# Attention and mixture-of-experts layer: value products by head parity, and the last group's values in three parts

## The reference, cut to what matters

```python
attn = jnp.einsum('bqhmd,bkhd->bhmqk', q, k) * sm_scale
attn = jnp.where(mask, -jnp.inf, attn)
w = jax.nn.softmax(jnp.concatenate([attn, sink], axis=-1), axis=-1)[..., :-1]
out = jnp.einsum('bhmqk,bkhd->bqhmd', w, v).reshape(B, L, NQ * HD)
x = x + out @ W_out
...
x = x + experts(layernorm(x))      # 8 experts, top 2, capacity 640
```

## Time and profile before

| | us |
|---|---|
| median of 3 runs | 1070.48 (1070.36 to 1070.66) |
| the profiled execution | 1065.58 |
| its span, first to last instruction | 1063.8 |
| PE busy | 1032.3 (97%) |
| DVE busy | 918.9 (86%) |
| value matmuls of all groups, PE busy | 247.9 |
| value matmuls of the last group | 793.16 to 800.32 |

### The profile page before, as it was taken

The page is one execution under the profiler, slowest core; times in us unless marked ns, Lnnn a source line. Parts: engine busy times, 40 slices in busy tenths (PEclk is TensorE's granted clock), DMA queues, the critical chain, the costliest instruction groups (busy, mean ns, idle before and its releaser), DMA issues.

```text
span 1063.8 us, 32339 instructions
## 1 busy us (share of the span) xinstructions
PE 1032.3 (97%) x13013; PEld 729.8 (69%) x13013; DVE 918.9 (86%) x1962; ACT 653.7 (61%) x1670; POOL 663.4 (62%) x607
## 2 busy tenths in 40 slices
PE   6899999999999999999999999999998999999996
PEld 4466666666666666666666666666566999999995
DVE  6999999999999999999999999999966777677773
ACT  4676667666667666667776656777654455544451
POOL 5657776767666888666777877667762422233332
PEclk8999999999999999999999999999999999999998
DMA  3544555544333344333343344333324344454421
GB/s 94 150 114 117 129 135 130 137 118 131 95 84 81 95 110 105 97 100 79 80 111 101 95 131 111 94 86 98 100 80 159 87 121 121 126 125 124 101 44 21
DMA packets 115574, 112.11 MB, mean 105 GB/s; under 512 B 35264, under 2 KB 103936, under 8 KB 115296
## 3 DMA queue, kind: packets, MB, share of 16 engines
q1 hardware_dynamic: 97648, 90.29, 31.3%
q0 software_dynamic: 7296, 8.55, 5.0%
q10 hardware_dynamic: 10480, 11.20, 3.8%
HBM read 74.84 MB, written 21.83 MB: 91 GB/s over the span
## 4 chain that ended last, share of the span: by engine, by line
PE 60%; DVE 35%; issue 2%; ACT 1%; DMA 0%; SPq 0%; POOLq 0%; DVEq 0%
PE bank L1536 21%; DVE probs_ring L1124 15%; DVE probs_t L1133 13%; PE bank L1701 11%; PE bank L1512 11%; PE bank L1712 7%; DVE heads_sb L1153 4%; PE bank L1715 4%; PE bank L1568 1%; PE bank L1441 1%; PE bank L1676 1%; PE bank L1458 1%; PE bank L1476 1%; PE bank L1596 1%; DVE neg_max L1124 0%
## 5 line engine op out<-in xcount | busy, mean ns | idle before, releaser
L841 ACT ACTIVATE probs_ring<-probs_ring,neg_max 128x512 f32<-128x512 f32 x512 | 365.9, 717 | 210.2 <-DVE neg_max L1124 209.4
L1124 DVE CUSTOM_DVE_ANT_0 probs_ring<-bank,mask,sink_neg 128x512 f32<-128x512 f32 x512 | 360.3, 738 | 24.9 <-PE bank L1512 23.8
L1133 DVE STREAM_TRANSPOSE probs_t<-probs_ring 128x1024 f32<-128x1024 f32 x256 | 317.8, 1241 | 0.2 <-ACT probs_ring L841 0.2
L1512 PE MATMUL bank<-qk_st 64*128 64x512 f32 x1024 | 280.6, 624 | 11.6 <-DVE neg_max L1124 7.4
L1536 PE MATMUL bank<-probs_t,v_quads 32*64 32x256 f32 x8192 | 247.9, 381 | 0.0
L1536 PEld LDWEIGHTS bank<-probs_t,v_quads 32*64 32x64 f32 x8192 | 179.3, 132 | 75.4 <-issue 48.1
L670 POOL TENSOR_TENSOR chunk_sb<-chunk_sb,rope_sb 128x512 f32<-128x512 f32 (+1 forms) x94 | 119.8, 1275 | 111.1 <-issue 80.6
L789 POOL DMA_INDIRECT out<-expert_sb,slots x40 | 77.8, 1945 | 150.6 <-DVE expert_sb L1385 143.3
L1512 PEld LDWEIGHTS bank<-qk_st 64*128 64x128 f32 x1024 | 85.3, 185 | 77.0 <-DVE neg_max L1124 41.5
L1043 ACT ACTIVATE hidden<-bank,b_sb 128x320 f32<-128x320 f32 x128 | 60.5, 524 | 107.1 <-PE bank L1701 107.1
L675 POOL TENSOR_TENSOR qk_st<-chunk_sb,swap_sb 128x512 f32<-128x512 f32 (+1 forms) x94 | 120.0, 1276 | 7.4
(11 more groups left out here) (189 smaller groups left out, 1352.5 us busy)
## 6 DMA issues: line engine op xcount, KB each, us to landing
v_quads<-v_rows SPq DMA_DIRECT2D x128, 128.0 KB
recip_wide<-recip_rows SPq DMA_DIRECT2D x64, 256.0 KB
w_raw<-in_L_ffn_w SPq DMA_DIRECT2D x14, 1024.0 KB, 8.2
swap_sb<-chunk_sb SPq DMA_DIRECT2D x314, 32.0 KB
w_raw<-in_L_attn_W_qkv SPq DMA_DIRECT2D x32, 256.0 KB, 2.9
slots<-slot_rows SPq DMA_DIRECT2D x9, 662.5 KB, 4.0
slot_rows<-x2T ACTq DMA_DIRECT2D x8, 662.5 KB, 6.2
w_raw<-in_L_attn_W_qkv SPq DMA_DIRECT2D x64, 64.0 KB, 2.7
```

Source lines behind the costliest of these rows:

```text
L841: nc.scalar.activation(probs[(g * UNITS + n) % RING][:, :], probs[(g * UNITS + n) % RING][:, :], ACT.Exp, bias=neg_max[j][:, n:n + 1], sca ...
L1124: nc.vector.tensor_tensor_reduce(probs[(g * UNITS + n) % RING][:, :], SCORE[SCORE_OF[n // 2][n % 2]][:, :], mask[:, L - P - t * P:2 * L - ...
L1133: nc.vector.transpose(probs_t[j][:, :, (h // 2) * (2 * P):(h // 2 + 1) * (2 * P)] .rearrange("p b (h q) -> p h b q", h=2)[:, :, :, t * BLK ...
L1512: nc.tensor.matmul(SCORE[SCORE_OF[n // 2][hh]][:, :], qk_st[j][half, h // 2, t * P:(t + 1) * P], qk_st[j][half, PAIRS, :], start=True, sto ...
```

## The change

Column halves are now the head within a pair (parity `h`), and the columns of a result are the pairs `c`. The moving operand of a matmul is therefore two pieces of 128 columns, 256 columns apart, where it was one piece of 256. The reciprocals, the view in which DVE makes the heads, and the load of `W_out` follow that layout.

In the last group the values are made in three parts, in columns 256 to 511 of the PV banks: pair 0 for queries 0 to 63 (the first quarter of the work) after the scores of step 10; in step 20, after the old rows of bank 2, pair 0 for queries 64 to 127, and pair 1 whole. The old rows of banks 1 and 0 follow. Queries 0 to 63 here are columns 0 to 63 of the 128 in a quarter, which are query tiles 0 and 1.

```diff
-                                 w_out.rearrange(...)[:, k, 2 * p:2 * p + 2, :]
+                                 w_out.rearrange(...)[:, k, p:p + 3:2, :]
...
-                    nc.vector.reciprocal(recip[:, 0:UNITS].rearrange("p (c h t) -> p c t h", c=PAIRS, h=2),
+                    nc.vector.reciprocal(recip[:, 0:UNITS].rearrange("p (h c t) -> p c t h", c=PAIRS, h=2),
...
+                    cols = slice(2 * P, 4 * P) if g == GROUPS - 1 else slice(0, 2 * P)
...
-                            PV[a][:, 0:2 * P].rearrange("p (h t i) -> p h t i", h=2, i=BLK),
+                            PV[a][:, cols].rearrange("p (c t i) -> p c t i", c=PAIRS, i=BLK),
...
             def pe_ahead(m):
+                if m == LAST + 10:
+                    pe.wait_ge(s_turned, LAST // 2 + 2)
+                    pe.wait_ge(s_v_in[1], (GROUPS // 2) * (16 * QUADS))
+                    pe.wait_ge(s_heads, 2 * (GROUPS - 1) + 1)
+                    last_values(0, slice(0, HD))
...
+            def values(g, j, blk, pairs, cols, q=slice(0, P)):
+                c, d = divmod(blk, TPB)
+                for a in range(QUADS):
+                    rows = slice(a * BLK, (a + 1) * BLK)
+                    probs_of = probs_t[j][rows, blk, :].rearrange("k (c h q) -> k c h q", c=PAIRS, h=2)
+                    for h in range(2):
+                        ins = nc.tensor.matmul(PV[a][h * HD:(h + 1) * HD, cols], v_quads[j][rows, d, c * HD:(c + 1) * HD],
+                                               probs_of[:, pairs, h, q], start=(blk == 0), stop=(blk == BLOCKS - 1))
+                return ins
+
+            def last_values(pair, q):
+                first = (2 + pair) * P
+                for blk in range(BLOCKS):
+                    ins = values(GROUPS - 1, 1, blk, pair, slice(first + q.start, first + q.stop), q)
+                return ins
...
                         pe.wait_ge(s_old_in, 16)
-                        for bank in (2, 1, 0):
+                        pe.wait_ge(s_neg_max, GROUPS * UNITS - 2)
+                        old_rows(2)
+                        pe.wait_ge(s_turned, GROUPS * (UNITS // 2))
+                        pe.wait_ge(s_y_out, 2 * g)
+                        last_values(0, slice(HD, P))
+                        last_values(1, slice(0, P)).then_inc(s_pv, 1)
+                        for bank in (1, 0):
                             pe.wait_ge(s_neg_max, GROUPS * UNITS - bank)
                             old_rows(bank)
...
-                    for blk in PV_AT[n]:
...
+                    if g < GROUPS - 1:
+                        for blk in PV_AT[n]:
+                            ins = values(g, j, blk, slice(0, PAIRS), slice(0, 2 * P))
+                        if blk == BLOCKS - 1:
+                            ins.then_inc(s_pv, 1)
```

More of the change, by code:

```diff
@@ L903, in load_wo @@
                     act.dma_start(wo_sb[p * HD:(p + 1) * HD, 2 * k:2 * k + 2, :],
-                                 w_out.rearrange("(k m d) n -> d k m n", m=QM, d=HD)[:, k, 2 * p:2 * p + 2, :]
+                                 w_out.rearrange("(k m d) n -> d k m n", m=QM, d=HD)[:, k, p:p + 3:2, :]
                                  ).then_inc(s_wo_in[k % 2], 16)
@@ L1151, in dve_step @@
                         dve.wait_ge(s_y, 2 * g + 1)
+                    cols = slice(2 * P, 4 * P) if g == GROUPS - 1 else slice(0, 2 * P)
                     for a in range(QUADS):
                         ins = nc.vector.tensor_tensor(
-                            heads_sb[:, a, :].rearrange("p (h t i) -> p h t i", h=2, i=BLK),
-                            PV[a][:, 0:2 * P].rearrange("p (h t i) -> p h t i", h=2, i=BLK),
-                            recip_wide[:, a, :].rearrange("p (h t i) -> p h t i", h=2, i=BLK), ALU.mult)
+                            heads_sb[:, a, :].rearrange("p (c t i) -> p c t i", c=PAIRS, i=BLK),
+                            PV[a][:, cols].rearrange("p (c t i) -> p c t i", c=PAIRS, i=BLK),
+                            recip_wide[:, a, :].rearrange("p (c t i) -> p c t i", c=PAIRS, i=BLK), ALU.mult)
                         if a % 2 == 1:
@@ L1520, in pe_step @@
                         pe.wait_ge(s_old_in, 16)
-                        for bank in (2, 1, 0):
+                        pe.wait_ge(s_neg_max, GROUPS * UNITS - 2)
[5 more added lines that the diff above has]
+                        for bank in (1, 0):
                             pe.wait_ge(s_neg_max, GROUPS * UNITS - bank)
                             old_rows(bank)
-                    if PV_AT[n][0] == 0:
+                    elif PV_AT[n][0] == 0:
                         pe.wait_ge(s_turned, g * (UNITS // 2) + UNITS // 2)
```

## The result

The changed kernel takes 1083.77 us (median of 4 runs, 1079.9 to 1086.01), the kernel before 1070.42 in the same session: ratio 1.0129, 95% interval 1.0093 to 1.0165. It is slower by 13.4 us. The forecast was no change, and the result lies above its range. The profiled execution took 1079.90 us; its span is 14.3 above that of before.

A forecast was written before the change was run, and what follows sets the result against it. PE, busy 97% of the span, was taken as the bound. Groups nothing, quarter 0.85 us late, values ending 1.4 us earlier, old rows moved behind them: -0.1 us, 1070.48 to 1070.4, no change; range 1069.4 to 1076.5.

The forecast's parts named there:

- the pace of the short matmuls: Last group's values: 7.0 ns a record of 64 columns, 13.8 ns a record of 128, against 27.5 for 256.
- q: Time of 256 records of 64 columns, in the mid-group quarter and again in step 20: 1.8 us each.
- r: Time of the 128-column records, pair 1 whole, in step 20: 3.5 us.
- a sign of being wrong: Profile after: short records' starts over 11 ns apart on average would show the forecast wrong.
- the prediction's own formula: Total difference for other paces: -0.1 + 2 (q - 1.8) + (r - 3.5) us.
- The reason for 7.0: In the last values' first 60 ns 8 matmuls and 8 loads started, under 8 ns a pair; lower pace chosen.
- Groups 0 to 30: Moving operand read in two pieces of 128 columns: costs nothing, 1 us kept to either side.
- The quarter's price in DVE's time: Quarter ahead of step 12's scores: scores +1.24 us, unit 14's mask, last transposes and reciprocals 0.85 us late.
- The end: After last transposes: values end 798.8 instead of 800.2, Y at 801.16 instead of 801.24; gain 0.5 us at most.
- The clock: Idle 1.5 us added before last values, one filled at 784: no loss taken; a fall would cost 1.7 us.
- Rival 1: Last group: PE's queue issues one matmul per 27.5 ns, q = r = 7.0, +13.8 us, 1084.3; chance 0.12.
- Rival 2: Last group: load not hidden under 64 columns, or middling instruction rate; q = r = 4.2, +5.4 us, 1075.9; chance 0.17.

The follow-up runs named there:

- All wide: Changed kernel with the last group's same 384 matmuls each streaming 256 columns instead of 64, 64 and 128; 1083.39 us, ratio 1.0114.
- two pairs: Changed kernel without the mid-group quarter: in step 20 pair 0 whole, then pair 1 whole, 256 matmuls of 128 columns; 1078.15 us, ratio 1.0067.
- values twice: Kernel with only the layout by parity, the last group's undivided values done twice in a row; 1080.05 us, ratio 1.0075.
- layout only: Changed kernel keeping only the layout by parity; last group's values undivided, 256 columns wide, behind all old rows as before; 1070.05 us, ratio 0.9972.
- Quarter, then whole: Changed kernel's mid-group quarter with its result thrown away, then all old rows and undivided values at step 20; 1074.27 us, ratio 1.0039.
- old rows behind Y: Layout by parity, undivided values, no quarter; old rows of banks 1 and 0 behind Y replace three unused matmuls; 1069.61 us, ratio 0.9994.
- the old rows between: Changed kernel with the old rows of banks 1 and 0 between step 20's 64-column and 128-column parts; 1081.22 us, ratio 1.0081.
- half a quarter: Changed kernel whose mid-group quarter takes only the first 8 of 16 key blocks, 128 matmuls of 64 columns; 1079.79 us, ratio 1.0086.

## Why the prediction was wrong

**What failed is the step "the pace of the short matmuls"**, q = 1.8 us and r = 3.5 us, worked out from what a tile needs and carried over to streams of 256 records. Two things were wrong in it, and the larger was a wait that it had put at nothing without a reason.

- *The supply.* The step took for granted that PE always has its next instruction. The cut takes the last group's value records from 256 to 768, 512 of them in step 20, and halves or better the time of each, so a block that lasted 3.5 us is used in 1.4 to 1.8. The pauses from start to start are 1.92, 2.10 and 3.53, 7.6 us together. "All wide" shows that the columns don't decide, "two pairs" that the same columns in twice the instructions take twice the time, with pauses 128 records apart, and "values twice" that the wide stream is itself at the limit. The page of before had the row for it, 103 packets and 1.69 MB of the queue "instruction", against 26,026 records of PE: some 250 instructions a packet could have been worked out and was not. So could the question how long the densest stretch of the trace of before was: 256 records in 7.16 us, nowhere faster for longer.
- *The pace itself.* At 2.4 GHz and away from the pauses the changed kernel's records of 64 columns start 11.2 ns apart in the mean (10.5 in the median) and not 7.0, which is over the 11 ns that the prediction gave as a sign of being wrong; those of 128 columns come at 14.2 in "two pairs" and not 13.8. So q is 2.9 us, and by the prediction's own formula this is -0.1 + 2 x 1.1 + 0.1 = +2.2 us, at the edge of what it called no change. The reason for 7.0, 8 pairs that start within 60 ns, holds for the first 8 of a stream, and the mean of a stream is another. The term was mis-sized, but the supply made the result.

**Groups 0 to 30: right.** Nothing; "layout only" has the same bursts to 0.01 us.

**The quarter's price in DVE's time: the mechanism was right, the size was not.** The prediction had +0.85 us at the last transposes. It is +5.66: the scores of step 12 start 5.08 us after the heads instead of 0.72, which is 4.36, and from those scores to the transposes' end it takes 9.29 instead of 7.99, 1.30 more. "Quarter, then whole" gives +4.97 with the clock up.

**The end.** Planned were 7.66 us from the transposes to Y, 17.80 came. Pauses are 5.63 of the difference and the longer stream 4.3, of which some 3 are the 128-column records that ran at 1.2 GHz (26.5 ns each and not 14.2). Full clock would have saved less than that: the next block landed at 807.65 and, by the 1.4 us seen elsewhere, could be used at about 809.05, so the last records would have ended near 810.2 instead of 811.14. This is an estimate, and it takes it that the block would not have come earlier. The behaviour of the old rows was right: from the last value to Y 2.51 us, planned 2.36, and the heads were not waited for. That this end can give 0.5 us at most was right too; "old rows behind Y" got 0.42.

**The clock: no fall was forecast, and it fell twice; the price was right.** The prediction had 1.7 us for a fall. The first cost 1.7: from the scores of step 12 to the last transposes' end it takes 9.29 us in the changed kernel and 9.30 with the old rows between, where the clock fell, and 7.60 or 7.61 in all wide, half a quarter and the thrown-away quarter, where it stayed up there. The second cost about 0.9 by the estimate above. Which stall brings it down the runs don't say: it fell in the changed kernel, with the old rows between, with two pairs and in step 20 of half a quarter, and not with all wide nor in the quarter that was thrown away. The pauses are there without the fall: the thrown-away quarter pauses for 2.9 us at full clock, and so do half a quarter and two pairs, at their first two block ends (2.30 and 3.32, 1.75 and 2.75 us from start to start; the clock fell at 800.48 and 797.60, behind them or at their end).

**The rivals.** Rival 1 gave 1084.3, 0.5 us from the result, and its reason is refuted: a record does not cost 27.5 ns however few columns it has. 222 records of 64 columns started within 2.58 us, 11.6 ns each, and 128-column ones come at 14.2. It is right only in the mean over the pauses, (4.94 + 15.4) / 768 = 26.5 ns, since the blocks arrive at 3.5 us and more. The rule of the Trainium skill that was weighed there (TensorE: Matmul & The Clock Gate, section "Wait — 56ns, not 53.3ns?"), no start to start below about 25 ns, does not hold for these matmuls on eight separate tiles: the measured 11.6 decides. Rival 2 had the right words in its heading, instructions that arrive at a middling rate, but priced them as a load per batch, +5.4. With a chance of 0.33 for slower and 0.61 for no change, the prediction looked at how long one short matmul takes and not at what 256 of them in a row ask for.

## What to carry to other kernels

Before a matmul is cut into narrower ones, count the instructions of the stretch and the time in which it is to use them up, and compare it with the densest stretch that the trace already has; the page's row of the instruction queue gives the size of a block. A cut that keeps the columns and doubles the instructions gains nothing once the stream is as dense as PE's supply, and loses a pause at every block. Idle time marked "issue" in the middle of one line, with a packet of the instruction queue landing in it, is the mark of this.

## What the runs showed of the hardware

- PE's instructions come during the run in packets of 16.4 KB, 256 instructions. Where PE had run dry it went on 1.2 to 1.5 us after the landing in all runs (1.36, 1.47 and 1.48 in the changed kernel, 1.19 in "quarter, then whole").
- The pauses that end after a packet's landing lie where a block ends, which is the same place of the program whatever the pace: behind 174, 302 or 430 records of step 20 in the changed kernel and its variants. Two kinds of delay lie elsewhere and stay without a cause: the 0.6 us behind 45 or 46 records of the quarter, and the 2 us in a usual group's 96 records of three runs. Which block's end PE stops at depends on the pace: 64 columns stop at 174, 256 columns ("all wide") go through it and stop 0.67 us at 302.
- While PE runs dry the packets start 3.4 to 5.8 us apart (797.22, 803.03, 806.73, 810.19 in the changed kernel; 797.07, 800.45 in half a quarter). What sets the longer distance stays open: data transfers filled the DMA engines in one pause (share 0.83 in 784.2 to 786.1) and were all but absent in another (797.9 to 799.9, share 0.01).
- The kernel before had such a pause too, which the prediction overlooked: in the value burst at 754.00 no weight load starts between 754.09 and 754.53, which is 1.47 us after a packet landed at 753.06. The burst is 0.5 us longer than others of its size.
